# Gated cross-attention and quantised FFN on one core: batches 1 to 3 attend and project with rounded high and low parts

## What is computed

```python
x = x + tanh(g_xattn[0]) * xattn(layernorm(x), ctx, w_sim, b_sim, W_qv, b_qv)
x = x + tanh(g_ffn[0])   * ffn(layernorm(x), w_gate, w_up, w_down)

def xattn(c, q, w_sim, b_sim, W_qv, b_qv):      # c: 4 x 1024 x 256, q: 4 x 154 x 256
    Sim  = (c @ w1)[:, :, None] + (q @ w2)[:, None, :] + einsum('bid,bjd->bij', c * w3, q) + b_sim
    A    = softmax(Sim, axis=2)
    hq   = einsum('bij,bjd->bid', A, q)
    hc   = einsum('bi,bid->bd', softmax(max(Sim, axis=2), axis=1), c)[:, None, :]
    return concatenate([c, hq, c * hq, c * hc], axis=-1) @ W_qv + b_qv
```

## Time and profile before

| quantity | value |
|---|---|
| median of 3 runs | 445.87 us (445.47 to 446.4) |
| profiled execution | 446.07 us |
| its span | 444.2 us |
| PE busy | 428.3 us, 96% of the span |
| DVE busy | 336.4 us, 76% |
| ACT busy | 290.0 us, 65% |
| POOL busy | 116.2 us, 26% |
| granted TensorE clock | full speed (2.4 GHz) in all 40 slices |

### The profile page before, as it was taken

The page is one execution under the profiler, slowest core; times in us unless marked ns, Lnnn a source line. Parts: engine busy times, 40 slices in busy tenths (PEclk is TensorE's granted clock), DMA queues, the critical chain, the costliest instruction groups (busy, mean ns, idle before and its releaser), DMA issues.

```text
span 444.2 us, 6830 instructions
## 1 busy us (share of the span) xinstructions
PE 428.3 (96%) x2432; PEld 294.7 (66%) x2432; DVE 336.4 (76%) x637; ACT 290.0 (65%) x376; POOL 116.2 (26%) x124
## 2 busy tenths in 40 slices
PE   4799999999999989999999999999999999999997
PEld 3688889988988878444444444444444444888886
DVE  5876669676574676884446799999988888997784
ACT  2577468667646254663443899996587778987750
POOL 1248435576749551100000024333000000000000
PEclk9999999999999999999999999999999999999999
DMA  7950002000200200200000000000000000334442
GB/s 235 327 183 0 1 2 94 2 1 2 94 1 0 96 1 2 94 0 0 0 0 1 0 0 0 1 0 1 0 0 0 0 0 23 120 123 141 142 142 72
DMA packets 20673, 21.14 MB, mean 48 GB/s; under 512 B 825, under 2 KB 20392, under 8 KB 20648
## 3 DMA queue, kind: packets, MB, share of 16 engines
q1 hardware_dynamic: 20628, 20.82, 14.8%
q10 hardware_dynamic: 20, 0.00, 0.0%
HBM read 12.43 MB, written 8.39 MB: 47 GB/s over the span
## 4 chain that ended last, share of the span: by engine, by line
PE 60%; issue 18%; DVE 14%; ACT 6%; DMA 1%; POOL 0%; ACTq 0%; POOLq 0%; DVEq 0%
PE ps L785 12%; PE ps L750 9%; PE ps L566 5%; PE ps L755 5%; PE ps L578 5%; PE ps L584 5%; PE ps L580 5%; DVE cols L1456 4%; PE ps L547 3%; DVE hid L1472 2%; ACT hid L1024 2%; PE ps L556 2%; PE ps L623 1%; PE ps L533 1%; PE ps L615 1%
## 5 line engine op out<-in xcount | busy, mean ns | idle before, releaser
L750 PE MATMUL ps<-xh,wuh 128*128 128x512 f16 x192 | 72.8, 379 | 0.8 <-DVE gq L1495 0.8
L750 PE MATMUL ps<-xh,wul 128*128 128x512 f16 x192 | 72.8, 379 | 0.0
L755 PE MATMUL ps<-xl,wuh 128*128 128x512 f16 x192 | 57.1, 379 | 0.0
L1435 DVE TENSOR_REDUCE cols<-hid x10 | 22.9, 2286 | 24.3 <-ACT hid L1001 24.3
L785 PE MATMUL ps<-wdh,oh 128*128 128x256 f16 x168 | 37.4, 273 | 0.0
L785 PE MATMUL ps<-wdl,oh 128*128 128x256 f16 x168 | 37.4, 273 | 0.0
L484 POOL PARTITION_ALL_REDUCE cols<-cols x4 | 1.5, 365 | 135.0 <-DVE cols L1395 129.2
L1001 ACT ACTIVATE hid<-ps 128x2048 f32 x10 | 18.7, 1875 | 27.5 <-PE ps L755 27.5
L750 PE MATMUL ps<-xh,wgh 128*128 128x512 f16 x96 | 36.4, 379 | 0.0
L750 PE MATMUL ps<-xh,wgl 128*128 128x512 f16 x96 | 36.4, 379 | 0.0
L750 PEld LDWEIGHTS ps<-xh,wuh 128*128 (+1 forms) x192 | 18.8, 98 | 24.1 <-issue 1.8
(11 more groups left out here) (225 smaller groups left out, 1009.7 us busy)
## 6 DMA issues: line engine op xcount, KB each, us to landing
x_scratch<-xa SPq DMA_DIRECT2D x4, 1024.0 KB, 4.4
xo<-x_scratch SPq DMA_DIRECT2D x16, 256.0 KB, 2.7
out_dram<-xo SPq DMA_DIRECT2D x15, 256.0 KB, 2.2
xa<-in_x SPq DMA_DIRECT2D x3, 1024.0 KB, 12.1
xa<-in_x SPq DMA_DIRECT2D x4, 256.0 KB, 4.9
wv<-in_L_xattn_W_qv SPq DMA_DIRECT2D x1, 1024.0 KB, 8.9
wr<-in_L_ffn_w_gate SPq DMA_DIRECT2D x1, 768.0 KB, 10.1
wr<-in_L_ffn_w_up SPq DMA_DIRECT2D x1, 768.0 KB, 11.4
```

The source lines that it names most:

```text
L750: pe.matmul(ps[hf][:, q, :], w_[:, d, ds(k * P, P)], xh[:, d, n], start=d == 0 and w_ is wh, stop=False)
L755: mm = pe.matmul(ps[hf][:, q, :], wh[:, d, ds(k * P, P)], xl[:, d, n], start=False, stop=d == KD - 1)
L1435: dve.tensor_reduce(gmx[:, ds(k * 2 + hf, 1)], unit(hid, k, hf), AX.X, ALU.max, apply_absolute_value=True).then_inc(gm_done, 1)
```

## The change

Three things are changed together.

1. Products with the attended tile are regrouped. `hqT @ W1` becomes `weights @ (context @ W1)`. A new `context_project` makes `context @ W1` once per batch (slots 6, 8, 12 and 14: `CW_AT`), with 4 float32 matmuls of 256 columns. The ACT copy to `hqT` is gone, and DVE makes `prT` straight from `hq_bank`.
2. In batches 1 to 3, `attend` and this projection use float32r operands: weights `ath`/`atl`, context `ch`/`cl` and projected context `cwh`/`cwl`, each a rounded high part and a low part that is the difference. Each product is high x high + high x low + low x high. The context rows are split into 122 (JM), with a matmul per term, and 32 (JR), whose three terms stand side by side in 96 rows (JS) of one matmul. Batch 0 keeps float32.
3. DVE's statistics of the new tile m+3 and of the result tile m-7 form one group in each slot (`both_stats`), and POOL does their arithmetic in four small instructions (`both_std`). The batch's own weights are, for batches 1 and 2, made by ACT (`batch_scaled`) and POOL (`batch_weights`); DVE keeps them for batches 0 and 3.

```diff
 PE, slot loop
-                if LAG <= m and not late:
-                    project(m - LAG, b - 1 if s == 1 and b < B else None)
-                if LAG <= m and late:
-                    project_first(b - 1)
+                if m == L + LAG:
+                    project_last()
+                elif LAG <= m:
+                    project_first(m - LAG)
+                    if s == 1 and b < B:
+                        batch_max(b - 1)
+                    if not late:
+                        project_rest(m - LAG)
+                if s == 3 and 1 < b < B:
+                    batch_cols(b - 1)
+                if m in CW_AT[1:]:
+                    context_project(CW_AT.index(m))
                 if m < N:
                     turn_h(m)
-                if s == 3 and b + 1 < B:
-                    turn_context(b + 1)
 ...
                     attend(m - 3)
+                if m == CW_AT[0]:
+                    context_project(0)
 PE, attend(n) for batches 1 to 3
+                    pe.wait_ge(al_rdy, n - NP + 1)
+                    pe.wait_ge(cl_rdy, b)
+                    pe.wait_ge(cr_rdy, b)
+                    pe.matmul(o_, ch[0:JM, par, 0, q], ath[0:JM, n % RA, 0, :], start=True, stop=False)
+                    pe.matmul(o_, ch[0:JM, par, 0, q], atl[0:JM, n % RA, :], start=False, stop=False)
+                    pe.matmul(o_, cl[b][0:JM, 0, q], ath[0:JM, n % RA, 0, :], start=False, stop=False)
+                    mm = pe.matmul(o_, ch[0:JS, par, 1, q], ath[0:JS, n % RA, 1, :], start=False, stop=True)
 PE, projection of the attended part for batches 1 to 3 (t = 0, 1)
+                pe.matmul(o_, ath[0:JM, n % RA, 0, q], cwh[0:JM, par, 0, :], start=start, stop=False)
+                pe.matmul(o_, ath[0:JM, n % RA, 0, q], cwl[0:JM, par, :], start=False, stop=False)
+                pe.matmul(o_, atl[0:JM, n % RA, q], cwh[0:JM, par, 0, :], start=False, stop=False)
+                mm = pe.matmul(o_, ath[0:JS, n % RA, 1, q], cwh[0:JS, par, 1, :], start=False, stop=False)
 PE, project_first(n)
+                if b == 0:
+                    pe.wait_ge(cwh_rdy, 1)
+                else:
+                    pe.wait_ge(cwl_rdy, b)
 PE, context_project(b), b > 0
+                    pe.wait_ge(ngm_rdy, b)
+                    pe.wait_ge(hc_rdy, min(b, 2))
+                    pe.wait_ge(cbi_rdy, min(b + 2, B))
+                    pe.wait_ge(cxr_rdy, b)
+                for o_, j in ((seen[0:JM, 0:D], slice(0, JM)), (seen[0:rest, D:2 * D], slice(JM, JM + rest))):
+                    for d in range(KD):
+                        mm = pe.matmul(o_, cxT[b % 2][:, d, j], wv[:, KD + d, :], start=d == 0, stop=d == KD - 1)
 DVE
+            def weights_low(n):
+                dve.wait_ge(aT_rdy, n + 1)
+                dve.tensor_tensor(atl[0:JM, n % RA, :], a_bank[0:JM, 0:PT], ath[0:JM, n % RA, 0, :].bitcast(F32), ALU.subtract)
+                rest = ath[2 * JR:JS, n % RA, 1, :]
+                dve.tensor_tensor(rest, a_bank[2 * JR:JS, PT:2 * PT], rest.bitcast(F32), ALU.subtract).then_inc(al_rdy, 1)
+            def both_stats(g):
+                dve.wait_ge(mv_done, g)
+                if g < N:
+                    for t in range(2):
+                        i_ = dve.bn_stats(st[:, t, :], xa[:, 2 * g + t, :])
+                if g >= YG:
+                    dve.wait_ge(x1_rdy, g - YG + 1)
+                    for t in range(2):
+                        i_ = dve.bn_stats(st[:, 2 + t, :], xa[:, 2 * (g - YG) + t, :])
+                i_.then_inc(bn_done, 1)
+                dve.wait_ge(bn_done, g + 1)
+                dve.wait_ge(std_rdy, g - 3)
+                for t in range(0 if g < N else 2, 2 if g < YG else 4):
+                    i_ = dve.bn_aggr(mv[:, g % 4, t, :], st[:, t, :])
+                i_.then_inc(mv_done, 1)
 ACT
-                if 3 <= m <= N + 2:
-                    attended(m - 3)
+            def batch_scaled(b):
+                act.wait_ge(hc_rdy, b + 1)
+                for d in range(KD):
+                    a_ = act.activation(we[:, b % 2, d, :], wv[:, 3 * KD + d, :], ACT.Copy, scale=c_hc[:, d:d + 1])
+                a_.then_inc(ws_rdy, 1)
 POOL
+            def both_std(g):
+                pool.wait_ge(mv_done, g + 1)
+                pool.tensor_scalar(vp[:, r, q], mv[:, r, q, 1], LN_EPS, 1.0, ALU.add, ALU.mult)
+                pool.tensor_scalar(nmean[:, r, q], mv[:, r, q, 0], -1.0, 1.0, ALU.mult, ALU.mult).then_inc(own_done, 1)
+                pool.tensor_tensor(rstd[:, r, q], vp[:, r, q], mhalf[:, q], ALU.pow).then_inc(own_done, 1)
+                pool.tensor_tensor(nmr[:, r, q], nmean[:, r, q], rstd[:, r, q], ALU.mult).then_inc(std_rdy, 1)
+            def batch_weights(b):
+                pool.wait_ge(ws_rdy, b)
+                pool.tensor_tensor(w_, w_, wv[:, 0:KD, :], ALU.add).then_inc(we_rdy, 1)
```

More of the change, by code:

```diff
@@ L41 @@
 J = 154
-JP = J // 2
+JR = 32
+JM = J - JR
+JS = 3 * JR
+RA = 5
 FF = 768
@@ L561, in attend @@
                 b, s, par = place_of(n)
-                pe.wait_ge(aT_rdy, n + 1)
-                ge(pe, hqT_rdy, n)
-                for d in range(KD):
-                    for k in range(2):
-                        mm = pe.matmul(hq_bank[:, d * PT:(d + 1) * PT], cx[b][0:JP, k, d * P:(d + 1) * P],
-                                       aT[0:JP, n % 3, k, :], start=k == 0, stop=k == 1)
-                mm.then_inc(hq_ps, 1)
-            def project(n, largest_of=None):
-                b, s, par = place_of(n)
+                ge(pe, pr_rdy, n)
@@ new lines, in project_product, with project_own @@
+            def project_product(n, t, o_):
+                b, s, par = place_of(n)
+                for d in range(KD):
+                    pe.matmul(o_, prT[:, par, d, s * PT + t * P:s * PT + (t + 1) * P], wv[:, 2 * KD + d, :], start=False, stop=False)
+            def project_own(n, t, o_, last):
+                b, s, par = place_of(n)
+                for d in range(KD):
+                    mm = pe.matmul(o_, hT[:, par, d, s * PT + t * P:s * PT + (t + 1) * P], we[:, par, d, :], start=False,
+                                   stop=last and d == KD - 1)
+                return mm
@@ L607, in project_rest @@
[L607 to L610 removed]
+                    project_attended(n, t, f_bank[n % 2][:, t * D:(t + 1) * D], t == 0)
+                for t in range(2):
+                    project_product(n, t, f_bank[n % 2][:, t * D:(t + 1) * D])
+            def project_rest(n):
+                pe.wait_ge(we_rdy, n // NP + 1)
                 for t in range(2):
[L612 to L615 removed]
+                    mm = project_own(n, t, f_bank[n % 2][:, t * D:(t + 1) * D], t == 1)
@@ L688, in _ @@
             pe.matmul(f_bank[1][:, D:D + 3], ones[0:1, :], row[0:1, D:D + 3], start=True, stop=True).then_inc(rows_ps, 1)
+            for t in range(2):
+                pe.transpose(a_bank[:, PT + t * P:PT + (t + 1) * P], ident[:], ident[:])
             turn_context(0)
@@ L1344, in _ @@
                     batch_max(b - 1)
+                if NP + 3 <= m <= N + 2:
+                    weights_low(m - 3)
+                if 4 <= m <= N + 3:
+                    attended(m - 4)
+                if m == N + 2:
+                    summary(b - 1)
+                    batch_weights(b - 1)
                 if m == 0:
@@ L1354, in _ @@
                     batch_shift(b - 1)
+                if s == 3 and 2 <= b < B:
+                    summary(b - 1)
                 if LAG < m:
@@ L1361, in _ @@
                     residual(m - LAG)
-                if 1 <= m < N:
+                if 1 <= m < LAG:
+                    scored(m - 1)
+                if 1 <= m and (m + 3 < N or LAG <= m) and not (LAG <= m and late):
+                    if s == 1 and m + 3 < N:
+                        dve.wait_ge(xr_in[b], 16)
+                    both_stats(m + 3)
+                if LAG <= m < N:
                     scored(m - 1)
```

410 lines of the change are left out of this document (226 added, 184 removed).

## The result

The changed kernel takes 456.93 us (median of 5 runs, 456.65 to 463.7) against 446.0 (445.47 to 446.4): a ratio of 1.0239, interval 1.0224 to 1.0253. It is slower by 10.9 us; the forecast was 437.7, in a range up to 446.0.

A forecast was written before the change was run, and what follows sets the result against it. PE was taken to bound the kernel before slot 19. Removing 20.7 us of its work, adding 6.9 and giving 5.6 back to late chains made -8.2 us: 437.7 us forecast, range 431.0 to 446.0.

The forecast's parts named there:

- float32r in place of float32: `attend` in slots 7 to 18, W1 part in 11 to 22: float32r matmuls pace 0.109 us, 20.7 us less.
- other cuts of batch 0: Context matmuls cut 122 + 32 instead of 77 + 77: nothing that can be told from zero.
- the start: Four more context transfers on the sync queue, ahead of batch 1's tokens: +0.3 us (0 to 1).
- PE's waits from slot 7 on: Time that late chains on other engines take back from PE's gain: 5.3 us more.
- the third rival: Float32r matmuls keep 0.216 us, or their weight load sets the pace at 190 ns: 453.8 us; chance 0.15.
- the fourth: The regrouping is float32 in effect, 0.43 us a matmul: about 495 us; within the third rival's chance of 0.15.
- Slots 6 and 7: PE waits 1.3 us (0.8 to 2) for ACT's copies of `context @ W1`; waits and a copy gone give -1.4.
- Slots 8 to 16: PE waits for `context_bias` in 8 and 12, +0.3 us; for `we` chains, +0.7 in 11 and +2.2 in 15.
- Slot 17: `yb` comes through `both_std`, queued behind POOL's row work, while PE's slot shrinks: +0.9 us (0 to 2).
- Slot 19: The 1.58 us wait for `yb` grows as PE's part shrinks and the chain hardly does: +1.3 us (0.5 to 2).
- The first: PE stays the bound everywhere, with waits only in slots 6, 7 and 19: 432.8 us; chance 0.15.
- The second: DVE and ACT become the bound; nine of slots 9 to 18 give back another 0.6 us each: 443.1 us; chance 0.20.

The follow-up runs named there:

- three-away kernel: Changed kernel with batch 0 cut 77 + 77, POOL's second weight normalization behind `both_std`, and DVE's score ahead of its statistics again: 446.47 us.
- experiment 3: Kernel before with the context rows cut 90 + 64, then 84 + 70, instead of 77 + 77: 455.41 us, then 446.08 us.
- experiment 5: Changed kernel with batch 0's context rows cut 77 + 77 instead of 122 + 32: 455.76 us.
- experiment 7: Changed kernel with the second weight's normalization moved behind `both_std` on POOL: 456.57 us.
- Experiments 2 to 4: Kernel before with context cut 122 + 32 (458.41 us), 90 + 64 (455.41), 84 + 70 (446.08), and 90 + 64 with equal-sized parts grouped in `attend` (449.46).
- experiment 6: Changed kernel with each 122-row context load made as two transfers of 112 and 10 rows: 457.28 us.
- experiment 9: Changed kernel with batch 0 cut 77 + 77 and the second weight's normalization moved on POOL: 450.44 us; with DVE's old order too: 446.47 us.
- Experiment 10: Three-away kernel with batch 0's `context @ W1` copied earlier, the third weight converted later on ACT, and `both_std` ahead of row sums on POOL: 442.57 us.

## Why the prediction was wrong

The gap between forecast (-8.2) and measured span (+12.6) by the prediction's own terms, in us:

| term | forecast | measured | from |
|---|---|---|---|
| float32r in place of float32 | -20.7 | -18.5 | slot 13: 9.50 to 7.96; slot 21, W1 part alone: 6.93 to 6.16 |
| `context_project` | +6.9 | +6.9 | slot 14 of the three-away kernel: 9.69 = 9.50 - 1.54 + 1.73 |
| other cuts of batch 0 | 0 | +5.8 | 4 x 0.68 for `attend` (experiment 3), 4 x 0.78 for the W1 part (slot 9 in experiment 5) |
| the start | +0.3 (0 to 1) | +2.5 | L774 at 7.54, before at 5.01 |
| PE's waits from slot 7 on | +5.3 | +9.8 | 12.2 - 2.4 |
| granted clock | 0 | +2.5 | `turn_y` of slot 19 to that of slot 20: 8.76 here, 6.21 in experiment 7 |
| left over | 0 | +3.6 | see below |

**Float32r: right, a little mis-sized.** Paces of 0.12 instead of 0.109 us, and 0.20 for the first of a group. Eight slots with both parts give 1.54 each and eight with one give 0.77 or 0.78: 18.5 instead of 20.7. The pace stays under the 0.151 us at which the third rival would decide, so it and the fourth are out. The recorded weight load of 190 ns didn't set the pace either.

**The step that failed most: "the other cuts of the context (122 + 32 instead of 77 + 77) are nothing I can tell from zero".** I counted instructions and columns and took rows for free. The trace of before has no instruction pair that goes from over 64 rows to 64 or fewer in a run of dense matmuls, so this was an operation that it didn't show, and I gave it neither bound nor rival. Experiments 2 to 4 show what it is: 0.15 to 0.17 us for each change. In the changed kernel that is 5.8 of the 20.8 us between forecast and measurement. The float32r part pays nothing of it, as its cuts are 122 and 96. The Trainium skill has a rule that fits ("TensorEngine Tiling (Array Packing)", Tiling Modes, Key Properties): changing the tiling mode drains the engine. The runs agree in that the price goes with the changes and not with the small tiles; that it is a drain, no run shows.

**The start.** I had counted the queue time of four more transfers and not their shape. The matmul on the row of 1 KB came 2.5 us later behind one transfer of 122 rows, and at 4.42 us behind 112 + 10. The Trainium skill ("DMA: Bandwidth & Descriptors", Why a DMA increments its semaphore by 16 and not by 1) says that a transfer runs on the largest number of engines, up to 16, that divides its outer dimension. By that rule it is an estimated 2 for 122 rows, and 16 for 112, 11 for 77, 15 for 90 and 14 for 84. The starts in experiment 6 agree with that; how the packets stood on the engines, no view here shows.

**Slots 6 and 7** were right in size: 0.82 us for `cw` where I had 1.3 (0.8 to 2), 1.76 once batch 0 is cut evenly. Of the gain I set against it (-1.4) the small waits before (0.61 for `we`, 0.21) did go, but 0.61 for `cxT` came in their place. So the two slots gave +0.6 in waits instead of -0.1.

**Slots 8 to 16.** The forecast had 0.3 for slots 8 and 12, 0.7 for slot 11 and 2.2 for slot 15. Measured: `we` in slot 15, 0.38 instead of 1.5, nothing in slot 11. But 1.14 and 1.26 before `weight_max` in slots 10 and 14, and 1.04 before `turn_a` in slot 14, where I had put nothing. I had written the engines' lists from the change and costed where PE waits for the statistics' results, but not that `scored` now stands behind them on DVE and what on PE waits for `scored`. Undoing the order alone gave 4 to 5 us back (experiment 9).

**Slot 17** was 1.97 instead of 0.9, at the upper bound of 2 and for the reason given: `both_std` behind other work on POOL. Experiment 10, which puts it ahead, takes the wait away.

**Slot 19** was 4.80 instead of 2.9. 2.5 of it is the collision of `we` on DVE with POOL's weight normalization, which before stood ahead of `we` in time and now beside it. Without it the wait is 2.30, inside the forecast of 1.58 + 0.5 to 2. The Trainium skill ("SBUF — State Buffer", SBUF: two separate sides) says that a VectorE instruction with two SBUF inputs and a GpSimd instruction that reads SBUF take a shared port pair in turn, each for a whole instruction. The trace agrees: 3.54 us until POOL's end, and 0.88 alone. I had costed both engines' lists by durations of undisturbed rows.

**The clock** wasn't in the sum: in the kernel before it is full behind all of PE's waits. The wait of 4.80 us was followed by 0.50 and 0.73 of the clock in the next two stretches, and cost 2.5 us more than itself (8.76 - 6.21, in the table). The length of the wait alone doesn't decide it. From slot 7 on, in the profiles of the changed kernel and its versions, the clock was at 0.50 within 3 us behind all three waits of 4.80 us and behind those of 3.65 (experiment 5) and 2.27 (experiment 10). It was so behind three of the six waits of 1.95 to 1.99 us in slot 17, and behind two of the seven of 0.82 or 0.83 in slot 7. Behind those of 2.30 and 2.31 us in slot 19 (experiments 7 and 9) it stayed at 1.00.

**The rivals.** The first (PE bound everywhere) is refuted by the waits. The second (DVE and ACT become the bound) came true in two slots, not as an even 0.6 us a slot but as order: the three-away kernel has these waits no more, with DVE busy for 335.0 us, where it was 336.4 before the change.

**Left over.** By the lengths of the slots, the 3.6 us lie in pieces of 0.2 to 0.7 us: 0.2 before slot 7, 0.4 in it, 0.5 in slot 12, 0.7 in slot 14 with its two waits, 0.2 in some others, and 0.45 in the FFN stage. In slot 11 the transposes of the context's 122 and 32 rows take 0.54 us instead of 0.27. I haven't traced the rest, and why the clock falls in one execution and not in the next is open too.

With batch 0 cut evenly and the orders on DVE, ACT and POOL mended, the changed kernel takes 441.81 us, 438.9 at full clock, against the 437.7 forecast. That doesn't confirm the forecast: this kernel has moves on three engines that the predicted one hasn't, and that it comes so near is in part luck.

## What to carry to other kernels

Cost a matmul by its rows too: when neighbouring float32 ones go between 70 or more and 64 or fewer rows, each change costs 0.15 to 0.17 us, three quarters of a 256-column float32 instruction. So keep both parts of a contraction above 64 rows, or group the small ones. When instructions are reordered on an engine, list for each one moved back who waits for it, not only for the ones moved ahead. And where a change brings PE a new wait, count on a slower clock behind it as a possible cost (2.5 us behind 4.80 us here), and look whether an easy move takes the wait away before keeping PE warm.

## What the hardware showed unasked

- Float32r at 122 or 96 rows and 256 columns: 0.12 us each, 0.20 for the first behind float32 instructions. Half a float32 matmul: 0.216. At the 1.2 GHz level a float32r one took 0.21 (experiment 7, 153.43 - 153.22).
- A change between float32 instructions of 90 or more rows and of 64 or 32: 0.15 to 0.17 us; none between 84 and 70; 32 and 64 rows cost the same (2.41 us for eight instructions in both).
- A transfer of 122 rows delayed the matmul that needs a 1 KB transfer of another queue by 2.5 to 3.1 us; 112 + 10 rows didn't.
- A float32 DVE instruction pair with two SBUF operands took 3.54 instead of 0.88 us beside a POOL instruction of 2.96 us.
- From slot 7 on TensorE's clock fell to the 1.2 GHz level behind every wait of 3.65 and 4.80 us, behind some of 0.82 to 2.27 us and not behind others of up to 2.31 us. It stayed at 2.4 GHz where spare transposes filled the longest wait.
